# Attention and FFN kernel: the slot scores from two rounded products instead of one in fp32

## The reference, cut to what matters

```python
x = x + xattn(layernorm(x), ctx_4096, ctx_4096, Wq, Wk, Wv, Wo, bo, g)      # 16 blocks of 128 x 1024
h = layernorm(x)
query = h @ Wq.T                                # 64 columns
rq, rk = query @ Wr.T, aux_keys @ Wr.T
router_scores = rq @ rk.T / sqrt(48) + log_rel  # 256 slots
top_scores, top_idx = top_k(router_scores, 8)
attn = query . aux_keys[top_idx] / sqrt(64) + log_rel[top_idx]
w = softmax(attn)
aux_out = (w @ aux_values[top_idx]) @ Wvd.T @ Wvu.T
gate = from var(h) and gelu(h @ Wu1.T + bu1) @ Wu2.T + bu2
out = x + h + gate * aux_out
```

## Time and profile before

| | |
|---|---|
| median of 3 runs | 623.61 us (620.17 to 623.72) |
| the profiled execution: its own time | 622.58 us |
| its span, first to last instruction | 620.8 us |
| PE busy | 592.5 us (95%) |
| PE weight loads busy | 516.5 us (83%) |
| DVE busy | 541.1 us (87%) |
| ACT busy | 418.1 us (67%) |
| POOL busy | 409.7 us (66%) |
| granted TensorE clock, mean | 0.996 |

### The profile page before, as it was taken

How to read it: one execution, slowest core, us unless ns; L and a number is a source line. 1 busy time by engine, 2 the same in 40 slices (tenths; PEclk the granted TensorE clock), 3 DMA queues, 4 the chain that set the end, 5 groups by cost and what they waited for, 6 DMA issues and landing times.

```text
span 620.8 us, 11452 instructions
## 1 busy us (share of the span) xinstructions
PE 592.5 (95%) x3718; PEld 516.5 (83%) x3718; DVE 541.1 (87%) x721; ACT 418.1 (67%) x864; POOL 409.7 (66%) x421
## 2 busy tenths in 40 slices
PE   4999999999999999999999999999989799999896
PEld 3778888888888888888888888888878799998574
DVE  5999999999999999999999999999968544866996
ACT  5566667676777676767676676777666576584783
POOL 4964457787767768687878787767655735430494
PEclk9999999999999999999999999999999899999999
DMA  8849695868687685959595868676563600000156
GB/s 315 223 128 231 189 248 167 216 180 207 188 201 212 171 231 154 243 173 242 162 243 169 219 179 204 197 195 175 134 196 109 180 8 2 2 2 0 59 214 271
DMA packets 63530, 106.11 MB, mean 171 GB/s; under 512 B 11392, under 2 KB 43680, under 8 KB 61168
## 3 DMA queue, kind: packets, MB, share of 16 engines
q1 hardware_dynamic: 52576, 84.32, 46.4%
q10 hardware_dynamic: 10000, 18.62, 13.2%
q0 software_dynamic: 896, 2.45, 1.3%
HBM read 46.62 MB, written 25.17 MB: 116 GB/s over the span
## 4 chain that ended last, share of the span: by engine, by line
PE 83%; DVE 4%; DMA 3%; ACT 3%; issue 3%; POOL 2%; ACTq 1%; DVEq 0%; SPq 0%; POOLq 0%
PE ob L548 18%; PE gm L517 16%; PE gm L604 5%; PE q_slot L475 4%; PE turn L501 4%; PE k_slot L477 4%; PE k_slot L475 4%; PE q_slot L477 4%; PE k_slot L476 4%; PE q_slot L476 4%; PE turn L604 4%; PE gm L526 2%; PE turn L559 2%; DMA Wuq_in<-Wuq_cols 2%; PE turn L734 1%
## 5 line engine op out<-in xcount | busy, mean ns | idle before, releaser
L1067 POOL TENSOR_TENSOR qs_sb<-qs_sb,qrec 128x1024 f32<-128x1024 f32 x64 | 122.0, 1906 | 96.3 <-DVE qrec L1257 96.1
L548 PEld LDWEIGHTS ob<-mt_sb,q_hd 128*128 128x128 f32 x1024 | 124.3, 194 | 8.3 <-ACT q_hd L805 3.0
L548 PE MATMUL ob<-mt_sb,q_hd 128*128 128x128 f32 x1024 | 127.9, 279 | 2.4 <-ACT q_hd L805 2.4
L517 PE MATMUL gm<-ekT,ctxT 128*128 128x256 f32 x512 | 118.2, 379 | 0.0
L517 PEld LDWEIGHTS gm<-ekT,ctxT 128*128 128x128 f32 x512 | 95.9, 190 | 13.6
L800 ACT ACTIVATE qs_sb<-qs_sb 128x1024 f32<-128x1024 f32 x64 | 67.9, 1061 | 47.3 <-DVE qs_sb L1246 45.9
L790 ACT ACTIVATE ek<-k_slot,nkm 128x1024 f32<-128x1024 f32 x62 | 69.1, 1114 | 32.7 <-DVE nkm L1221 32.5
L1221 DVE TENSOR_REDUCE nkm<-k_slot 128x1 f32<-128x1024 f32 x62 | 74.0, 1194 | 13.9 <-PE k_slot L477 13.9
L1253 DVE TENSOR_REDUCE qsum<-qs_sb 128x16 f32<-128x1024 f32 x64 | 77.1, 1205 | 7.6 <-ACT qs_sb L800 6.5
L1246 DVE TENSOR_TENSOR qs_sb<-q_slot,qm 128x1024 f32<-128x1024 f32 x64 | 78.4, 1224 | 2.2
L1228 DVE STREAM_TRANSPOSE kt<-ek 128x1024 f32<-128x1024 f32 x64 | 79.0, 1234 | 1.1 <-DMA ekT<-kt 1.1
(11 more groups left out here) (208 smaller groups left out, 1309.9 us busy)
## 6 DMA issues: line engine op xcount, KB each, us to landing
ekT<-kt SPq DMA_DIRECT2D x488, 64.0 KB, 2.9
q_turned<-qt SPq DMA_DIRECT2D x16, 1024.0 KB, 4.8
q_hd<-q_turned ACTq DMA_DIRECT2D x64, 256.0 KB, 5.7
ctx_in<-ctx_rows SPq DMA_DIRECT2D x16, 512.0 KB, 6.1
x_all<-x SPq DMA_DIRECT2D x16, 512.0 KB, 4.7
ctxT<-ctx_cols SPq DMA_DIRECT2D x16, 512.0 KB, 5.5
out<-q_hd SPq DMA_DIRECT2D x15, 512.0 KB, 2.6
Wuq_in<-Wuq_cols ACTq DMA_DIRECT2D x1, 1280.0 KB, 9.3
```

Source lines behind the costliest of these rows:

```text
L517: last = nc.tensor.matmul(gm[:, cols], ctxT[:, b % 2, j, :], ekT[:, 2 * half:2 * half + 2, :, j * BLK:(j + 1) * BLK], start=(j == 0), stop ...
L548: last = nc.tensor.matmul(ob[:, (j % 4) * C:(j % 4 + 1) * C], q, mt_sb[:, b % 2, t, :], start=(t == 0), stop=(t == T - 1))
L1067: nc.gpsimd.tensor_tensor(e, e, qrec[:, i % 2, :].unsqueeze(2).broadcast_to([P, PAIR, DH]), ALU.mult).then_inc(q_mul, 1)
```

## The change

The fp32 product of a score becomes two rounded products that add up in PSUM. The first multiplies `query` by `score_hi`, the rounded table; `query` now holds the rounded query in rows 0 to 63 and its rest (what rounding took away) in rows 64 to 127, and `score_hi` holds the same rounded table in both halves. The second multiplies `query_one` (rounded query in rows 0 to 63, ones below) by `score_lo`: the table's rest in rows 0 to 63, and in rows 64 to 127 log_rel, rounded in row 64 and its rest in row 96, zeros else. For this: the keys and Wr are passed twice, so that `scoreB` fills 128 rows; `query_rows` writes the 64 columns twice; `query_copy` is three instructions instead of one; `score_tables` is new on DVE, ahead of hidden step 10; log_rel goes by four SP DMAs into `log_rows` (it lies over `logits`) instead of two POOL DMAs into `scoreB`; POOL's clears are for `log_rows` and `query_one` at b = 17 in place of `scoreB` and `q_rows`; `qt` and `xn` move into the part of SBUF that FFN uses again.

```diff
@@ -80,11 +80,9 @@
         qs_sb = sb("qs_sb", [P, 2, N])
-        qt = sb("qt", [P, len(BY_BLOCKS), N])
         junk = sb("junk", [P, 4, C])
...
         o_sb = sb("o_sb", [P, 2, J, C])
-        xn = sb("xn", [P, N])
         bo_bc = sb("bo_bc", [P, C])
@@ -112,6 +110,8 @@
         att = ExitStack()
+        qt = sb("qt", [P, len(BY_BLOCKS), N], scope=att)
+        xn = sb("xn", [P, N], scope=att)
         ctx_in = sb("ctx_in", [P, N], scope=att)
@@ -137,12 +137,15 @@
         WvdT = stage2[:, 2 * N:2 * N + HD].rearrange("p (j d) -> p j d", j=J)
-        keysT = stage2[0:BOT, 2 * N + HD:2 * N + HD + NSLOT]
+        keysT = stage2[0:P, 2 * N + HD:2 * N + HD + NSLOT]
         WrT = stage2[0:BOT, 3 * N:3 * N + RDIM]
-        Wr_in = stage2[0:RDIM, 3 * N + 64:3 * N + 64 + BOT]
+        Wr_in = stage2[0:RDIM, 3 * N + 64:3 * N + 64 + P]
         rkT = stage2[0:RDIM, 3 * N + 256:3 * N + 256 + NSLOT]
         ffn = ExitStack()
+        query_one = sb("query_one", [P, B, C], F32R, ffn)
+        score_hi = sb("score_hi", [P, 2 * NSLOT], F32R, ffn)
+        score_lo = sb("score_lo", [P, 2 * NSLOT], F32R, ffn)
@@ -153,7 +156,7 @@
         units = sb("units", [P, 2, UH], scope=ffn)
-        query = sb("query", [P, B, C], scope=ffn)
+        query = sb("query", [P, B, C], F32R, ffn)
         WvuT_in = sb("WvuT_in", [P, N], scope=ffn)
@@ -183,6 +186,7 @@
         ffn.close()
+        log_rows = logits[:, :, :].rearrange("p k s -> p (k s)")
         y_out = q_hd
@@ -260,7 +264,10 @@
         score_ready = sem("score_ready")
-        score_zeros = sem("score_zeros")
+        log_zeros = sem("log_zeros")
+        score_high = sem("score_high")
+        score_split = sem("score_split")
+        query_high = sem("query_high")
@@ -425,6 +432,10 @@
                     sp.dma_start(dst, src).then_inc(ffn_in, 16)
+                sp.wait_ge(log_zeros, 1)
+                for row in (BOT, BOT + BLK):
+                    for n in range(2):
+                        sp.dma_start(log_rows[row:row + 1, n * NSLOT:(n + 1) * NSLOT], log_rel_row).then_inc(log_rel_in, 16)
                 sp.dma_start(WvuT_in[:, :], WvuT_raw).then_inc(wvu_in, 16)
@@ -576,12 +587,12 @@
                 pe.wait_ge(table_in, 16 * TABLES)
-                nc.tensor.matmul(ob[0:RDIM, NSLOT:2 * NSLOT], WrT, keysT, start=True, stop=True).then_inc(rk_prod, 1)
+                nc.tensor.matmul(ob[0:RDIM, NSLOT:2 * NSLOT], WrT, keysT[0:BOT, :], start=True, stop=True).then_inc(rk_prod, 1)
...
                 pe.wait_ge(rk_copied, 1)
-                nc.tensor.matmul(ob[0:BOT, 0:NSLOT], Wr_in, rkT, start=True, stop=True).then_inc(b1_prod, 1)
+                nc.tensor.matmul(ob[:, 0:NSLOT], Wr_in, rkT, start=True, stop=True).then_inc(b1_prod, 1)
@@ -614,7 +625,9 @@
                     pe.wait_ge(masked, b - 1)
-                nc.tensor.matmul(score_psum(b), query[:, b, :], scoreB[:, :], start=True, stop=True).then_inc(scores, 1)
+                nc.tensor.matmul(score_psum(b), query[:, b, :], score_hi[:, :], start=True, stop=False)
+                nc.tensor.matmul(score_psum(b), query_one[:, b, :], score_lo[:, :], start=False,
+                                 stop=True).then_inc(scores, 1)
@@ -638,13 +651,13 @@
                         pe.wait_ge(o_copied, 2 * B)
-                        pe.wait_ge(query_ones, 1)
                     if b == EARLY + 5:
...
                 if b == B - 2:
-                    pe.wait_ge(log_rel_in, 16 * 2)
+                    pe.wait_ge(score_split, 4)
+                    pe.wait_ge(query_ones, 1)
                     for n in range(2):
@@ -974,12 +987,11 @@
                         nc.scalar.copy(rkT, ob[0:RDIM, NSLOT:2 * NSLOT]).then_inc(rk_copied, 1)
-                        act.wait_ge(score_zeros, 1)
-                        nc.scalar.mul(scoreB[0:BOT, NSLOT:2 * NSLOT], keysT,
+                        nc.scalar.mul(scoreB[:, NSLOT:2 * NSLOT], keysT,
                                       float(BOT) ** -0.5).then_inc(score_ready, 1)
...
                         act.wait_ge(b1_prod, 1)
-                        nc.scalar.mul(scoreB[0:BOT, 0:NSLOT], ob[0:BOT, 0:NSLOT],
+                        nc.scalar.mul(scoreB[:, 0:NSLOT], ob[:, 0:NSLOT],
                                       float(RDIM) ** -0.5).then_inc(score_ready, 1)
@@ -1119,8 +1131,6 @@
             pool.wait_ge(consts, 2)
-            nc.gpsimd.memset(scoreB[BOT:P, :], 0.0).then_inc(score_zeros, 1)
-            pool.wait_ge(score_zeros, 1)
             def move_k(half):
@@ -1139,8 +1149,6 @@
                 move_k(half)
-            for n in range(2):
-                nc.gpsimd.dma_start(scoreB[BOT:BOT + 1, n * NSLOT:(n + 1) * NSLOT], log_rel_row).then_inc(log_rel_in, 16)
             for b in range(PERIODS):
@@ -1168,7 +1176,12 @@
                             pool.wait_ge(k_moved[half], moved(B))
-                        nc.gpsimd.memset(q_rows[:, :, BOT:P], 1.0).then_inc(query_ones, 1)
+                    if early_step(b, i) == 0:
+                        pool.wait_ge(g_prod, 2 * B)
+                        pool.wait_ge(m_prod, B)
+                        nc.gpsimd.memset(log_rows[:, :], 0.0).then_inc(log_zeros, 1)
+                        pool.wait_ge(q_written, 16 * B)
+                        nc.gpsimd.memset(query_one[:, :, :].bitcast(F32), 1.0).then_inc(query_ones, 1)
                     if early_step(b, i) > 0:
@@ -1293,11 +1306,30 @@
             def query_rows(b):
-                V.tensor_copy(q_rows[:, b, 0:BOT], unit_psum(b)[:, UH:UQ]).then_inc(rows_copied, 1)
+                V.tensor_copy(q_rows[:, b, :].rearrange("p (r d) -> p r d", r=2),
+                              unit_psum(b)[:, UH:UQ].unsqueeze(1).broadcast_to([P, 2, BOT])).then_inc(rows_copied, 1)
...
                 dve.wait_ge(rows_T, b + 1)
-                V.tensor_copy(query[:, b, :], query_psum(b)).then_inc(query_done, 1)
+                V.tensor_copy(query[:, b, :], query_psum(b)).then_inc(query_high, 1)
+                dve.wait_ge(query_high, b + 1)
+                if b == 0:
+                    dve.wait_ge(query_ones, 1)
+                V.tensor_copy(query_one[0:BOT, b, :], query[0:BOT, b, :].bitcast(F32))
+                V.tensor_tensor(query[BOT:P, b, :], query_psum(b)[BOT:P, :], query[BOT:P, b, :].bitcast(F32),
+                                ALU.subtract).then_inc(query_done, 1)
+
+            def score_tables():
+
+                dve.wait_ge(log_rel_in, 16 * 4)
+                V.tensor_copy(score_hi[:, :], scoreB[:, :]).then_inc(score_high, 1)
+                V.tensor_copy(score_lo[BOT:P, :], log_rows[BOT:P, :]).then_inc(score_split, 1)
+                dve.wait_ge(score_high, 1)
+                V.tensor_tensor(score_lo[0:BOT, :], scoreB[0:BOT, :], score_hi[0:BOT, :].bitcast(F32),
+                                ALU.subtract).then_inc(score_split, 1)
+                dve.wait_ge(score_split, 2)
+                V.tensor_tensor(score_lo[BOT + BLK:P, :], log_rows[BOT + BLK:P, :], score_lo[BOT + BLK:P, :].bitcast(F32),
+                                ALU.subtract).then_inc(score_split, 2)
@@ -1477,6 +1509,8 @@
                     V.tensor_copy(WvuT_hi[:, :], WvuT_in[:, :]).then_inc(wvu_hi, 1)
+                if b == EARLY + 2:
+                    score_tables()
                 if b == EARLY + 4:
@@ -1540,9 +1574,9 @@
         "WvuT_raw": np.concatenate([a["L0_ffn_Wvu"].T] * 2, axis=0),
-        "keysT_raw": a["L0_ffn_aux_keys"].T,
+        "keysT_raw": np.concatenate([a["L0_ffn_aux_keys"].T] * 2, axis=0),
         "WrT_raw": a["L0_ffn_Wr"].T,
-        "Wr_raw": a["L0_ffn_Wr"],
+        "Wr_raw": np.concatenate([a["L0_ffn_Wr"]] * 2, axis=1),
         "bu1_row": row("L0_ffn_bu1"),
```

## The result

| | before | after |
|---|---|---|
| median of the runs | 622.52 us (4 runs beside the changed kernel) | 635.23 us (4 runs, 632.47 to 635.58) |
| ratio, with its 95% interval | 1 | 1.0199 (1.0154 to 1.0244) |
| profiled execution: time, span | 622.58, 620.8 us | 635.58, 633.7 us |
| mean granted clock of TensorE in it | 0.996 | 0.979 |

The changed kernel is 2% slower. The forecast was 627.5 us with a range to 631.5; the time lies outside it, on the side of rival 1 and beyond that rival's own price (about 630).

The account below looks back on a forecast made before the run. PE, DVE and POOL were taken to stand at the same pace in the closing rounds, PE only just slowest. +2.5 +0.6 +0.2 +1.3 -0.4 = +4.2, less 0.3 at the end: +3.9, 627.5 us; range 623.0 to 631.5.

Parts of the forecast that it names:

- rival 1: Waits at step 11 and the hand-over lower TensorE's granted clock: +5.7 to +7.4 us, about 630; chance 0.25.
- PE's saving: Scores on PE: 0.39 us saved each, 6.3 over sixteen, of which only 0.4 us shows, through POOL's closing additions.
- Rivals 3 and 4: Scores: 3, PE's saving counts in full, 6.3 us, 617.3, chance 0.05; 4, rounded form saves nothing, 628.2, chance 0.05.
- rival 2: The lock misses score_tables and ACT's tail absorbs the rest: +2.1 us, 625.7; chance 0.18.
- the lock: In score_tables, POOL's sum goes between the two subtractions and holds DVE's second for 1.03 us.
- Step 11: score_tables on DVE makes hT_low(11) late, so PE waits for it before the 24 products: +2.5 us.
- The clock: TensorE's granted clock behind the new waits: taken to stay at full speed, as after the earlier 2.25 us gap.
- Query, 0.69 us each: Three DVE operations per query, starts +0.32, +0.15, +0.22: 0.69 us each, 1.38 for two, against 0.39 before.
- Step 13, "0.2 more": PE's logtotal waits for query 7 from DVE: 0.2 us more; a lock on query 6, 1.1, left to the range.
- the delay of ACT's chain: ACT's casts up to h_scale(14) run late, so PE's transposes of block 14 wait: 0.6 us more.
- Hand-over, +1.3: Before the closing rounds DVE finishes the last queries later, and PE's first closing transpose waits for them: +1.3 us.
- The tail, -0.3: At the end, DVE's wait for PE before block 15 goes because PE now runs ahead: 0.3 us off.

Follow-up runs that it names:

- products_only: Changed kernel without the split of query and table: one table cast at step 4, one copy per query, two rounded products per score; 622.15 us, ratio 0.9989.
- filler: Changed kernel with spare products on PE, 20 ahead of its wait for hT_low(11) and 28 ahead of the last query copy; 631.97 us, ratio 1.0132.
- tables_step4: Changed kernel with the score table's operations moved from hidden step 10 to step 4; 631.29 us, ratio 1.0120.
- pool_one: Changed kernel with the score table at step 4 and the lower query copies made by GpSimd instead of VectorE; 624.21 us, ratio 1.0029.
- after_q6: Changed kernel in which PE's sum of the logarithms waits for query 6 only, not query 7; 632.57 us, ratio 1.0144.
- after_again: The changed kernel, unedited, run once more for a second profile; median 634.23 us, ratio 1.0187.

## Why the prediction was wrong

**PE's saving: right.** Two rounded products 0.23 us apart, 0.47 for a score; POOL's pairs 4.85 us, its twelve additions 0.3 us shorter for 0.4 forecast; no sign of the 6.3 us. products_only shows this part by itself. Rivals 3 and 4 are out, and rival 2 as well, for the lock came. The step left out one thing: less work on PE means a longer idle time ahead of its next wait.

**Step 11: the mechanism was right, the size too small.** Forecast +2.5 for the later start of the products; it was +3.3, of which PE idled 2.97 us. The train from score_hi's start to hT_low(11)'s took 3.30 us for 3.06 forecast (2.4 and 0.9 of lock, for 2.03 and 1.03), and it began 0.4 us later after step 9's end than forecast (3.95 us instead of 3.5), for the queries ahead of it. The lock came inside the table as forecast, though on its first subtraction and not on the second.

**The clock: the first step that failed.** Rival 1 put it at 0.25 and priced it for step 11 and the hand-over; the forecast took it as absent on the strength of one row, the 2.25 us wait that it had survived. It fell behind the wait of step 11 in all three profiles of kernels that have this wait in full and nothing to fill it (waits of 2.97, 2.98 and 2.97 us), and behind the hand-over's in every kernel with the split queries and no spare products there. The Trainium skill says as much of products behind a long wait ("TensorE: Matmul & The Clock Gate", "HAM oscillation — how this bites in real kernels"), and these waits agree with it. The row of 2.25 us had spoken against a fall, and it was the weaker witness, as the forecast itself had 2.5 and 4.1 us for the new waits. In step 11 it costs 1.5 us (filler takes it away, and nothing else in that step changes), in the hand-over 0.6 to 1.1 (1.3 in products_only). Rival 1 as it was priced, +5.7 to +7.4, does not reach the measured +9.6 and +11.9 behind step 9 either: the rest is VectorE's queries, in the next three points, and the tail.

**Query, 0.69 us each: wrong term.** Measured 0.88, as the start of each of the three operations follows the last at 0.32, 0.23 and 0.33. The forecast had 0.32, 0.15 and 0.22: it let the second and the third overlap with the next one, as the copies in the earlier trace rows do, and measured they don't; each starts only when the one before it has ended. It is not that each needs the one before it (the lower copy and the subtraction both need the rounded query, but not each other). L1368 of the kernel before, which like the subtraction works on rows 64 to 127, didn't overlap either: 0.29 us, and the next start 0.32 or 0.33 later. That the change between lower and upper rows is the reason is a guess that no run tests. For two that is 1.76 us instead of 1.38.

**Step 13, "0.2 more": the second step that failed, as large as the clock of step 11.** The forecast saw the wait for query 7 and gave it 0.2 us, with 1.1 for a lock "left to the range", and then said that the delay of ACT's chain would take 0.6 ahead of it. Measured: the ACT chain added nothing (the transposes of block 14 began 5.06 us after the end of step 11's products in both kernels), and the wait for query 7 cost 1.8 us, with the lock on query 6, and 3.4 where the clock fell behind it. tables_step4 has step 13 at its longest without step 11's delay (there ACT's block came later as well, 0.90 us of wait instead of 0.23), pool_one and after_q6 take it away from either side. In the forecast's own terms the 0.2 was mis-sized by 1.6 us, and the 0.6 ahead of it, for ACT's chain, did not come. tables_step4 shows that the wait does not need the delay of step 11 at all: two queries and their rows cost DVE 1.4 us more in every step, and that, with the lock, is enough.

**Hand-over, +1.3: the size was off by half.** From the end of step 14 to the last query VectorE needs 11.5 us instead of 9.3, +2.2. Up to unit_bias(15) it is +0.9 for 0.27 forecast: queries 10 to 13 cost 0.88 each, and PE's transposes of 12 and 13 wait 0.42 and 0.58 us for VectorE. From there to the last query it is +1.3 for 1.07. Behind it, the clock, +0.6 (in filler, where the clock stays up, the stretch from the first closing transpose to POOL's first addition is 7.29 us, as before with 7.27; in the changed kernel it is 8.02).

**The tail, -0.3: wrong in sign.** It is 0.5 longer. The forecast read VectorE's last instruction before, at 615.62, as held by PE; it follows its own predecessor, which starts at 614.42 and takes 1.28 us. Now VectorE waits 1.65 us for block 11's output to be stored, and its last instruction starts 3.5 us after POOL's last addition has ended:

```profile
628.45 1.41 DVE L1409 SCALAR_TENSOR_TENSOR q_hd<-q_slot,oscale,x_all 128x512 f32<-128x512 f32 x2 [1.65 <-DMA out<-q_hd]
```

In tables_step4, filler and after_q6 this is 3.4 to 3.7 us and the tail as long; in products_only and the four kernels with POOL's query copies the tail is 8.1 us, as before (2.7 us in pool_one). Why the store lands later where VectorE makes those copies is open; no run here tells.

**How it adds up.** Behind step 9 the first profile has +9.6 us for +3.9 forecast. Of the 5.7 us between them the clock is 2.1 (1.5 and 0.6), VectorE's queries and table are 2.7 (0.8 at step 11, 1.0 at steps 12 and 13, 0.9 at the hand-over), the tail 0.8 and POOL's additions 0.1; the second profile adds 1.5 of clock at step 13. By the medians, against 1.0193 for the changed kernel (mean of 1.0199 and 1.0187): the table off step 10, 1.0120; the copy below off VectorE, 1.0029; the shorter wait and the filled one, 1.0002. So about 4.5, 5.7 and 1.7 us, and nothing left beyond the last interval of 1.7 us to either side; the last of the three steps alone is within the noise. The first two are not independent: with light queries the table's place costs 3.4 us. The forecast had 2.5 to 3.3 us for the table and 1.3 for the queries (1.5 with step 13's 0.2); it was the queries that it undersold.

## What to carry to other kernels

Work taken off the engine with the highest busy share is worth what the next pace-setter leaves, here 0.3 us of 6.3 (POOL 2.42 us and VectorE 2.30 a block behind PE's 2.45), while each 0.2 us put on an engine whose queue others wait for is paid at every such wait. When a change is costed, a new wait on TensorE as long as the forecast ones should carry the price of the clock with it (1.5 us for 24 products here), as the likely case and not as a rival: at step 11 and at the hand-over the clock fell behind every idle wait of 2.95 us and more and stayed up behind the four of 2.10 to 2.27 us. A one-time preparation belongs where its engine waits anyway: the same four operations cost 3.4 to 4.5 us at step 10 and nothing at step 4 that stands out of the variation of what lies before step 9.

## What the runs showed of the hardware

- **The clock did not go by the length of the last wait alone.** At step 13 it fell behind waits of 0.23 and 1.58 us (after_again) and stayed up behind 0.23 and 1.56 of the same kernel (after) and behind 0.49 and 1.56 (filler), with the same work between them. At step 11 it fell behind 2.97 and stayed up behind 2.27; at the hand-over it stayed up behind 2.10 to 2.25 in three profiles and fell behind 2.95.
- **An execution of one and the same kernel varies by 1.3%, and much of it lies in one stretch.** Twenty-five runs of the kernel before on one chip took 619.74 to 628.07 us; step 9 ended up to 5.6 us apart in thirteen profiles of eleven kernels, with granted clocks of 0.5 to 1.0 between 465 and 496 us. A ledger of two profiles has to be checked against a second execution before a term of some 3 us is believed.
- **POOL and VectorE as casters.** A cast of 64x1024 within SBUF took POOL 1.04 us, one of 64x256 0.40; the same 16 queries one by one took VectorE 0.23 us each, and query 6 0.65 to 0.74 more, where POOL's block sum had come first (five profiles).
